# A transformer block on one core: the opening in half groups and chunks, 13 products on a cleared tile, and statistics and norms one group later in VectorE's order

## What is computed

```
xn = (x - mean(x)) / sqrt(var(x) + 1e-5)                  # over the 256 features
Q, K, V = xn @ Wq + bq, xn @ Wk + bk, xn @ Wv + bv        # 16 heads of 16
attn = softmax(Q K^T / 4 + alibi)                         # 1024 x 1024 for each head
out = x + (attn V) @ Wo + bo
    + sum over the top 2 of 8 experts (router xn @ Wg):  w * (silu(xn W1) * (xn W2)) W3
    + (silu(xn Ws1) * (xn Ws2)) Ws3                       # shared expert
```

## Time and profile before

| what | value |
|---|---|
| median of 3 runs | 2366.53 us |
| lowest and highest | 2364.92 and 2369.34 us |
| span of the profiled execution | 2364.1 us |
| busy: PE, DVE, ACT, POOL | 2329.9, 1985.7, 1712.9, 1012.0 us |
| granted TensorE clock, mean | 0.998 |

### The profile page before, as it was taken

The page is one execution under the profiler, slowest core; times in us unless marked ns, Lnnn a source line. Parts: engine busy times, 40 slices in busy tenths (PEclk is TensorE's granted clock), DMA queues, the critical chain, the costliest instruction groups (busy, mean ns, idle before and its releaser), DMA issues.

```text
span 2364.1 us, 51756 instructions
## 1 busy us (share of the span) xinstructions
PE 2329.9 (99%) x19966; PEld 1561.3 (66%) x19966; DVE 1985.7 (84%) x3243; ACT 1712.9 (72%) x3279; POOL 1012.0 (43%) x1013
## 2 busy tenths in 40 slices
PE   7999999999999999999999999999999999999998
PEld 6874444444444444444444448999999989988998
DVE  7889999999999999999999956777777765555555
ACT  4447889888999999999999987777777763333332
POOL 2112556553225555454454324343433354455444
PEclk9999999999999999999999999999999999999999
DMA  8984545543224444343443325777777753344432
GB/s 304 379 323 171 168 157 163 160 147 95 83 86 133 121 128 131 111 127 120 117 127 113 106 92 177 234 244 238 238 245 234 245 179 107 108 124 128 123 107 90
DMA packets 189750, 383.15 MB, mean 162 GB/s; under 512 B 54164, under 2 KB 100756, under 8 KB 176292
## 3 DMA queue, kind: packets, MB, share of 16 engines
q1 hardware_dynamic: 151536, 219.17, 28.9%
q0 software_dynamic: 36880, 159.87, 21.1%
q10 hardware_dynamic: 1088, 0.79, 0.1%
HBM read 247.86 MB, written 140.31 MB: 164 GB/s over the span
## 4 chain that ended last, share of the span: by engine, by line
PE 87%; DVE 8%; DMA 2%; issue 1%; ACT 1%; SPq 1%; POOL 0%; DVEq 0%; POOLq 0%; ACTq 0%
PE ps L534 84%; DVE mx L1010 5%; PE ps L547 3%; DVE mx L1013 2%; DMA Md<-mT 1%; SPq L1516 0%; ACT qkH L829 0%; DMA OPS<-Md 0%; DMA xr<-Xn 0%; ACT pta L849 0%; DMA xt<-in_x 0%; DVE qkL L1000 0%; ACT accs L856 0%; POOL rstd L1224 0%; DVE xn L984 0%
## 5 line engine op out<-in xcount | busy, mean ns | idle before, releaser
L1010 DVE TENSOR_REDUCE mx<-ps 128x1 f32<-128x512 f32 x1552 | 959.5, 676 | 4.9 <-PE ps L534 4.5
L534 PE MATMUL ps<-OPS 52*128 52x512 f32 (+1 forms) x4096 | 749.3, 446 | 4.8 <-DMA OPS<-Md 1.9
L534 PEld LDWEIGHTS ps<-OPS 54*128 54x128 f32 (+1 forms) x4096 | 359.0, 184 | 463.5 <-ACT pta L849 209.9
L849 ACT ACTIVATE pta<-ps 128x512 f32<-128x512 f32 x1024 | 541.1, 598 | 79.6 <-PE ps L534 71.9
L849 ACT ACTIVATE ptb<-ps 128x512 f32<-128x512 f32 x1024 | 536.3, 600 | 45.5 <-PE ps L534 37.6
L534 PE MATMUL ps<-OPS,WB 128*128 128x256 f32 (+2 forms) x2364 | 384.4, 315 | 3.1 <-DVE VB L1135 1.6
L534 PEld LDWEIGHTS ps<-OPS,WB 128*128 128x128 f32 (+1 forms) x2364 | 332.3, 182 | 28.2 <-issue 3.9
L534 PE MATMUL ps<-pta,VB 128*32 128x352 f32 (+1 forms) x4096 | 300.6, 388 | 0.1
L1013 DVE TENSOR_REDUCE mx<-ps 128x2 f32<-128x1024 f32 x248 | 300.2, 1210 | 0.2 <-PE ps L534 0.2
L534 PE MATMUL ps<-ptb,VB 128*32 128x352 f32 (+1 forms) x4096 | 300.2, 388 | 0.0
L1268 POOL TENSOR_SCALAR m<-m 128x16 f32<-128x16 f32 x64 | 16.9, 265 | 558.8 <-DVE m L1023 558.8
(11 more groups left out here) (171 smaller groups left out, 2865.8 us busy)
## 6 DMA issues: line engine op xcount, KB each, us to landing
OPS<-QKh SPq DMA_DIRECT2D x512, 64.0 KB
Xs<-zero POOLq DMA_DIRECT2D x71, 256.0 KB, 3.6
xr<-Xs SPq DMA_DIRECT2D x71, 256.0 KB, 5.3
Ys<-VB SPq DMA_DIRECT2D x71, 256.0 KB, 5.0
QKh<-qkH SPq DMA_DIRECT2D x16, 1024.0 KB, 7.3
QKl<-qkL SPq DMA_DIRECT2D x16, 1024.0 KB, 8.9
OPS<-QKl SPq DMA_DIRECT2D x256, 64.0 KB
asum<-Sd SPq DMA_DIRECT2D x64, 256.0 KB
```

Source lines behind the costliest of these rows:

```text
L534: return self.e.matmul(o, l, r, start=start, stop=stop)
L849: self.e.activation(pt(m)[:, half * GT:(half + 1) * GT], ps[:, n % 3, :], ACT.Exp).then_inc(sem["exp"], 1)
L1010: self.e.reduce_max(mx[:, r % 2, hh, i, half:half + 1], ps[:, bank, :], AX.X).then_inc(sem["mxred"], 1)
```

## The change

1. **Clearing and warm products.** DVE clears half of the tile `XL` (128x1024) first of all, and PE runs 13 products of 512 columns on it, before the first data is there. Their result is not used.
2. **Group 0 in halves and chunks.** x of group 0 comes in two transfers, and statistics, power and norms go by halves. The transposes wait for each half; the copy to XH and the rest XL go by chunks of 512 columns, each with its own semaphore, and the first unit has its products in another order, so that it starts with the first chunk of XH.
3. **Weights.** The split of Wq, Wk, Wv and Wo, one step before, becomes four; the low part of Wv moves from DVE to POOL. The bias is scaled before the split of Wk, and Wo is split during group 0.
4. **The order from group to group.** In `run`, group g's statistics were taken with group g - 3, the norms of g with g - 2 and its columns ahead of the units of g - 1. Now the statistics are taken with group g - 2 (at o = 4 and 5), the norms with group g - 1 (at o = 0 and 1), and the columns with group g - 1 behind the third qk unit (o = 2).

```
+            def warm_up(self):                        # Tensor
+                self.w.wait_ge("wz", 1)
+                for i in range(WARM):
+                    self.mm(ps[:, 4, :], XL[:, 1, 0, 0:P], XL[:, 1, 1, :], True, True)
...
         for g in range(NG):
-            if g + 3 < NG:
-                self.stats(g + 3, 0)
-            if g + 2 < NG:
-                self.norm(g + 2, 0)
-            if 0 < g and g + 1 < NG:
-                self.columns(g + 1)
             self.pad(g + 1)
...
-                if o == 1 and g + 2 < NG:
-                    self.norm(g + 2, 1)
-                if o == 3 and g + 3 < NG:
-                    self.stats(g + 3, 1)
+                if o == (1 if g == 0 else 0) and g + 1 < NG:
+                    self.norm(g + 1, 0)
+                if o == 1 and g + 1 < NG:
+                    self.norm(g + 1, 1)
+                if o == (4 if g == 0 else 2) and g + 1 < NG:
+                    self.columns(g + 1)
+                if o == 5 and g == 0:
+                    self.split_wo()
+                if o in (4, 5) and g + 2 < NG:
+                    self.stats(g + 2, o - 4)
...
+            def first_unit(self):
+                out_q = ps[:, self.project_bank(0), :]
+                wh, wl = (Wqk[k][:, 0, :, 0:P] for k in ("h", "l"))
+                self.w.wait_ge("xhf", 1)
+                self.mm(out_q, wl[:, 0, :], XH[:, 0, 0, :], True, False)
+                self.mm(out_q, wh[:, 0, :], XH[:, 0, 0, :], False, False)
+                self.w.wait_ge("xh", 1)
...
+            def scale_bias(self):                     # Vector
+                self.w.wait_ge("c_w", 64)
+                self.e.tensor_scalar(bqk[:, 0:2], bqk[:, 0:2], SCALE, None, ALU.mult).then_inc(sem["bq"], 1)
...
-                self.load_x(0)
+                e.dma_start(xt[:, 0, 0:2, :], x_v[0][:, 0:2, :]).then_inc(sem["x0f"], 16)
+                e.dma_start(xt[:, 0, 2:4, :], x_v[0][:, 2:4, :]).then_inc(sem["x0"], 16)
```

More of the change, by code:

```diff
@@ L87, in run @@
         self.begin()
-        self.stats(0, 0)
-        self.stats(0, 1)
+        self.warm_up()
+        for half in range(2):
+            self.stats(0, half)
         for half in range(2):
             self.norm(0, half)
-        self.split_weights()
+        self.split_q()
         self.columns(0)
-        self.stats(1, 0)
-        self.stats(1, 1)
-        self.split_wo()
+        self.scale_bias()
+        self.split_k()
+        for half in range(2):
+            self.stats(1, half)
+        self.split_v()
         self.pad(0)
[L98 to L101, removed]
         n = 0
@@ L286, in stats, with warm_up, split_q, split_k @@
     def stats(self, g, half): pass
-    def split_weights(self): pass
+    def warm_up(self): pass
+    def split_q(self): pass
+    def split_k(self): pass
+    def split_v(self): pass
+    def scale_bias(self): pass
     def norm(self, g, half): pass
@@ L551, in columns @@
                 w.wait_ge("c_ident", 16)
+                if g == 0:
+                    for half in range(2):
+                        w.wait_ge("norm", half + 1)
+                        for c in range(2):
+                            for j in (2 * half, 2 * half + 1):
+                                q = self.turn(ps[:, c, j * P:(j + 1) * P], xn[:, 0, j, c * P:(c + 1) * P])
+                            if half:
+                                q.then_inc(sem["xt" if c else "xtf"], 1)
+                    return
                 w.wait_ge("norm", 2 * g + 2)
@@ L571, in project_qk @@
                 k, c0 = g % 2, (o % 2) * P
+                self.w.wait_ge("wspll", o // 2 + 1)
+                if g == 0 and o == 0:
+                    self.first_unit()
+                    return
                 self.w.wait_ge("xh", g + 1)
                 self.w.wait_ge("xl", g + 1)
-                self.w.wait_ge("wspll", 3)
                 bank = self.project_bank(8 * g + o)
@@ L979, in norm @@
                 k, n = g % 2, g % 3
-                self.w.wait_ge("rstd", g + 1)
+                if g == 0 and half == 0:
+                    self.w.wait_ge("rsf", 1)
+                else:
+                    self.w.wait_ge("rstd", g + 1)
                 self.w.wait_ge("xt", g - 2)
@@ L990, in columns @@
                 self.w.wait_ge("vmm", 4 * (g - 1))
+                if g == 0:
+                    for c, (done, low) in enumerate((("xhf", "xlf"), ("xh", "xl"))):
+                        self.w.wait_ge(done, 1)
+                        self.e.tensor_tensor(XL[:, 0, c, :], ps[:, c, :], XH[:, 0, c, :].bitcast(F32), ALU.subtract
+                                             ).then_inc(sem[low], 1)
+                    return
                 self.w.wait_ge("xh", g + 1)
```

95 lines of the change are left out of this document (64 added, 31 removed).

## The result

| what | before | after |
|---|---|---|
| median, 7 runs of each on one chip | 2365.81 us | 2371.53 us |
| lowest and highest | 2364.92 and 2369.34 | 2369.65 and 2375.3 |
| ratio, with its 95% interval | | 1.0023, 1.0013 to 1.0032 |
| the profiled execution: own time, span | not given, 2364.1 | 2369.65, 2367.8 |
| granted clock, mean | 0.998 | 0.998 |

The ratio is 5.4 us, 3.1 to 7.6 by its interval: slower, and the bound of 4.7 us for what a measurement can tell lies inside that interval. The profiled execution is 3.7 us longer. I had forecast 2.3.

A forecast was written before the change was run, and what follows sets the result against it. PE's queue was taken to bound the kernel, DVE also full behind the projections. Terms -8.2 + 5.0 + 1.9 + 1.5 + 2.1 = +2.3 us: span 2366.4, about 0.1% longer, no measurable change; range 2363.5 to 2373.5.

The forecast's parts named there:

- The opening, 8.2 earlier: Start of the kernel: group 1's first product at 21.6 instead of 29.80, so 8.2 us ahead.
- the contention with POOL: Opening: group 1's norms run beside POOL's subtraction and are slowed; 0.4 us added, between nothing and 0.6.
- Groups 1 to 4, 5.0 lost: Each of groups 1 to 4 takes 11.10 instead of 9.85, 1.25 us lost four times.
- the two waits that I named: PE idle in groups 1 to 4: 1.09 us for the next group's norms, 0.5 for the fourth unit's qkL.
- Groups 5 to 12, 1.9; 13, 1.5; 14, 2.1: Later groups' losses: 0.24 us in each of 5 to 12, 1.5 in 13, 2.1 in 14.
- Comes out at the end one for one: Whatever is gained or lost up to the last projection reaches the kernel's end in full, both engines being full behind.
- The 2.4 between span and median: Whole kernel: 2.4 us added to the forecast span of 2366.4, taken from the earlier span 2364.1 and median 2368.8.
- The products cost nothing: Opening: the 13 warm products end between 6.2 and 7.4, ahead of the last transposes at 7.65; cost nothing.
- The clock did not stay low: Rival for the opening: PE's clock stays at the lower level, 1.6 us more, 2370.4; chance 0.15.
- bv was 0.7 late: Slower rival, opening: the bias transfer lands late, each us costing one; three us more gives 2371.8; chance 0.17.
- PE did wait for the norms: Faster rival denied this: groups without maxima take 10.0, with them 10.7; -6.4 us, 2360.1; chance 0.08.
- what I called slower: Whole kernel: a measured time longer by more than about 0.2%, 4.7 us; chance 0.17.

The follow-up runs named there:

- e9: The changed kernel run again, nothing altered, one profiled execution: 2374.83 us.
- e3: Changed kernel with the low part of Wv subtracted on DVE, not POOL: 2372.23 us, ratio 1.0018 to the kernel before.
- e1: Changed kernel with the columns behind the fourth qk unit (o = 3), not the third, from group 1 on: 2361.88 us, ratio 0.9978 to the kernel before.
- e2: Changed kernel without the clearing and the 13 warm products: 2368.52 us, ratio 1.0009 to the kernel before.
- e6: e5 without the clearing and the warm products: 2358.26 us, ratio 0.9972 to the kernel before.
- e5: Changed kernel with columns at o = 3, Wv low on DVE, bias between statistics halves, last groups' statistics and norms ahead of dense maxima: 2358.63 us, ratio 0.9964.
- e4: Changed kernel with only the order from group to group put back as before: 2370.52 us, ratio 1.0014 to the kernel before.
- e13: Kernel before with only its columns moved behind the fourth qk unit, same edit as e11, second run: 2363.43 us, ratio 0.9987.
- e8: The kernel before run again, nothing altered, one profiled execution: 2368.57 us.
- e11: Kernel before with only its columns moved behind the fourth qk unit, first run: 2364.24 us, ratio 0.9983.

## Why the prediction came out as it did

The time was inside my range, 2.7 over the forecast; the sign of the small difference was right, and its size was taken for half of what it is.

- **The opening, 8.2 earlier: the mis-sized term.** It is 6.6 in one trace and 7.4 in the other. The mechanism was right: DVE's list with the bias behind the transfer of bv. I had put the landing at 11.5 and the first qkL at 14.1. In e9 they are 11.39 and 14.02, as forecast; in the first trace 12.24 and 14.86. So 0.8 of the 1.6 missing there is the landing's scatter, within the bounds that I had given, and passes on in full. The other 0.8 is in both traces. For the contention with POOL I added 0.4 to four norms, taking as a slowdown of 0.3 a pair. They show a hold: of that pair's 1.01 the first norm has 0.69, from 21.06 to 0.14 behind the clearing's end at 21.61. Read so, the price is POOL's end less the norm's start, and the chain of subtraction and two clearings makes 2.20 for one norm, 1.8 over the 0.41 of one alone. From the first qkL to group 1 it took 8.34 in both traces and 6.85 in e3, where the hold is 1.49 shorter: the hold passes on in full. I had 7.1 for that stretch without any contention, so the other steps were some 0.5 too long and hid a part of it. The landing of the second half of x was wrong too (5.66 and 5.32, not 4.47), and the power of half a group took 0.72 and 0.79, not 1.04, but DVE had time ahead of the bias.
- **Groups 1 to 4, 5.0 lost.** 5.3 measured, from 23.20 to 67.86 against 29.80 to 69.13 before. Groups 2 to 4 took 11.04 where I said 11.10, by the two waits that I named. Group 1 took 11.55: the first norm of a pair began 0.1 ahead of a clearing on POOL and took 0.76, until 0.15 behind its end, and PE's wait for the norms was 1.19 and not 0.87. The two waits of groups 2 to 4 are 0.87 and 0.33; I had 1.09 and 0.5.
- **Groups 5 to 12, 1.9; 13, 1.5; 14, 2.1.** Measured 1.8, 1.56 and 2.10. e1 shows the mechanism of the first.
- **"Comes out at the end one for one".** From group 15 to the end of attention it did within 1 us (4.14, then 4.35, then 3.22 later than before). Behind that one execution is no measure: a clock dip near 205 costs some of them 1.0 to 2.7, and the start of the experts varies by 3 us and more. I had made the sum against a single span and taken the rest of the kernel as fixed. The 2.4 between span and median was no constant either: in every timed execution on record the time is 1.75 to 1.93 over its own span, so 0.6 of the 2.4 was scatter between executions. The trace gives 4.1 where the runs give 5.4 (3.1 to 7.6), and that difference stays within what these two places can do; it was not traced further.
- **"The products cost nothing".** Right by e2 and e6. What they bring is 1.0 at group 1 between the traces of e5 and e6, nothing between e2 and the changed kernel, and nothing in any median.
- **The rivals.** The clock did not stay low: the first unit's products are 0.23 apart. bv was 0.7 late in one trace and 0.1 early in the other, not 3. PE did wait for the norms. The interval of the ratio reaches over 0.2%, so what I called slower is as near to the truth as no change, but by the hold and by what happens behind attention, and not by the mechanism of that rival. That the range of 10 us holds the result says little: the trace at group 15 (4.14, 3.20) supports the sum of 2.3 to within 2 us, and the 5.4 of the medians was reached in part by stretches that I had not looked at.

## What to carry to other kernels

Count, for each engine that others wait for, what stands ahead of the first thing they wait for: in e4 the data came as early as in the changed kernel, and the first qkL 6.9 us later, since the order of DVE was the old one. When a step is moved to save latency once (in the opening), check what it costs in each of the sixteen rounds; the better place was one unit further on (e1: 5 us under the kernel before, not 5 over it). For differences of 0.2% read a point in the trace ahead of the stages that vary, beside the medians, and neither alone; and take a second trace of the same kernel before a microsecond is given a cause, since here one transfer alone moved that point by 0.8.

## What the hardware showed that I had not expected

- A norm on DVE (128x256, scalars by partition) that begins beside POOL's work is held until 0.14 or 0.15 behind POOL's end, however long that is: 2.20 beside a subtraction and two clearings, 1.84 beside a subtraction and one (e4, 15.69 to 17.52, POOL done at 17.38), 0.71 and 0.69 beside clearings, where one alone takes 0.41. The powers on POOL held no norm (7.13 to 7.53 beside 6.98 to 7.77, 0.41), and DVE's qkL, which overlaps one too (14.86 beside 15.01), showed nothing of it. The Trainium skill ("GPSIMD Engine Reference", section 8) names DVE's instructions with two SBUF inputs or in a two-port mode as those that contend. These norms have one tensor input; the trace doesn't say in which mode they ran.
- The clock rose 1.4 to 1.8 us after the first product in e2, 4.0 to 4.3 after it in e6, though both had 2.03 of transposes ahead and the same products. In the kernel before, with 1.94 of transposes, it rose 5.3 after the first product (13.60), and in e13, with the same instructions up to there, 3.6. The Trainium skill ("TensorE: Matmul & The Clock Gate", Part 4) states that transposes don't count as activity; these traces neither bear it out nor refute it.
- PE idle for 2.44 us in the opening kept the clock, and so did 2.84 (e8); after 3.20 (e11) and 3.23 (e13) it fell a microsecond after work began again, and after 8.24 (e4) it was low at once. Near 205 us no such pause stands ahead: the longest idle stretch of PE between 190 and 205 is 1.2 us in e13, 0.97 in e11, 1.05 in e8 and 1.02 in the kernel before, and the clock fell in the first three and not in the last.
- One transfer of x in two halves brought the second half 1.2 us (0.85 in e9) later than the whole had come, and the first half 0.6 earlier (3.89).
